# A store of mixed tokens and a weight load move ahead of a store in the SyncE queue of an AdaLN and FFN kernel

## The reference, cut to what matters

```python
# layer 0: grouped 9-tap convolution + context bias, then an int8-quantised matmul
y  = conv1d(x, L0_weight, groups=4) + cond @ c_weight.T + bias
x1 = x + int8_matmul(quantise(y), quantise(L0_ffn_weight)) * scales      # per row
# layer 1: a 64x64 channel mix per batch, then a dense FFN and a gated rank-32 term
x2 = einsum('boi,bih->boh', agg_w[b], x1) + agg_b
H  = x2 @ W.T + b ;  z = x2 @ A
out = x1 + H + (z * gates(H, z)) @ Bmat * scaling
```

## Time and profile before

| | us |
|---|---|
| median of 3 runs (lowest, highest) | 614.74 (613.66, 615.96) |
| the profiled execution | 616.81 |
| its span, first to last instruction | 615.0 |
| PE / DVE / ACT / POOL busy | 599.2 / 434.6 / 356.9 / 374.8 |
| DMA: moved, mean rate | 136.24 MB, 222 GB/s |

### The profile page before, as it was taken

The page is one execution under the profiler, slowest core; times in us unless marked ns, Lnnn a source line. Parts: engine busy times, 40 slices in busy tenths (PEclk is TensorE's granted clock), DMA queues, the critical chain, the costliest instruction groups (busy, mean ns, idle before and its releaser), DMA issues.

```text
span 615.0 us, 16175 instructions
## 1 busy us (share of the span) xinstructions
PE 599.2 (97%) x6467; PEld 343.3 (56%) x6500; DVE 434.6 (71%) x883; ACT 356.9 (58%) x622; POOL 374.8 (61%) x252
## 2 busy tenths in 40 slices
PE   8999999989999999999999999999999999999998
PEld 4656766667767777676554444444444444444444
DVE  5978999978999999997788667654535454355543
ACT  3879998889999999976644343544243333321100
POOL 3326555447766666655797946889877659656200
PEclk8999999999999999999999999999999999999999
DMA  8979988778999898783074115855455346532111
GB/s 339 351 207 297 382 306 295 266 273 299 332 322 328 323 320 314 262 309 139 37 284 163 34 45 193 314 206 194 172 182 200 118 164 237 207 141 99 70 68 69
DMA packets 38632, 136.24 MB, mean 222 GB/s; under 512 B 5036, under 2 KB 5580, under 8 KB 38513
## 3 DMA queue, kind: packets, MB, share of 16 engines
q1 hardware_dynamic: 33518, 118.43, 54.7%
q10 hardware_dynamic: 5040, 16.78, 6.8%
HBM read 87.95 MB, written 47.24 MB: 220 GB/s over the span
## 4 chain that ended last, share of the span: by engine, by line
PE 86%; issue 2%; DVE 1%; ACT 0%; DVEq 0%
PE ps L909 41%; PE ps L612 15%; PE ps L517 9%; PE ps L709 7%; PE ps L596 4%; PE ps L891 2%; PE ps L581 2%; PE ps L657 2%; PE ps L652 1%; PE ps L621 1%; PE ps L625 0%; PE ps L692 0%; DVE yb L1459 0%; PE ps L677 0%; ACT zT L1097 0%
## 5 line engine op out<-in xcount | busy, mean ns | idle before, releaser
L612 PE MATMUL ps<-wqT,yq_both 128*128 128x512 bf16 x479 | 115.2, 378 | 5.6 <-issue 4.6
L1284 POOL TENSOR_TENSOR x<-x_in,f_all 128x512 f32<-128x512 f32 x64 | 74.3, 1161 | 49.4 <-DVE f_all L1496 49.2
L1288 POOL TENSOR_TENSOR x_split<-x_ph,x_split 128x1032 f16<-128x1032 f32 x25 | 53.7, 2148 | 55.5 <-ACT x_split L995 55.5
L1022 ACT ACTIVATE yv<-yb,yinv 128x128 f32<-128x128 f32 x256 | 77.8, 388 | 0.8 <-DVE yinv L1487 0.8
L1323 POOL TENSOR_TENSOR ring<-ring 128x512 f32<-128x512 f32 x56 | 72.7, 1299 | 4.3
L612 PEld LDWEIGHTS ps<-wqT,yq_both 128*128 128x128 bf16 x512 | 45.5, 99 | 46.0 <-issue 1.2
L1496 DVE SCALAR_TENSOR_TENSOR f_all<-ps,tok_scale,wsc_b 128x512 f16<-128x512 f32 x64 | 47.9, 749 | 18.8 <-PE ps L612 17.9
L517 PE MATMUL ps<-x_split,conv_h 128*64 128x256 f16 (+1 forms) x1248 | 60.1, 274 | 0.0
L517 PEld LDWEIGHTS ps<-x_split,conv_h 128*64 128x64 f16 (+1 forms) x1248 | 47.5, 108 | 9.8 <-issue 7.9
L1816 DVE SCALAR_TENSOR_TENSOR x_in<-ps,unscale,x_in 128x512 f32<-128x512 f32 x30 | 22.5, 750 | 39.9 <-PE ps L909 39.8
L1816 DVE SCALAR_TENSOR_TENSOR wst<-ps,unscale,wst 128x512 f32<-128x512 f32 x27 | 20.3, 750 | 36.7 <-PE ps L909 36.7
(11 more groups left out here) (351 smaller groups left out, 1322.2 us busy)
## 6 DMA issues: line engine op xcount, KB each, us to landing
x_in<-in_x SPq DMA_DIRECT2D x32, 512.0 KB, 6.1
x_scratch<-x SPq DMA_DIRECT2D x32, 512.0 KB, 3.6
x_ph<-in_x_phases SPq DMA_DIRECT2D x31, 516.0 KB, 5.1
x_scratch<-ring SPq DMA_DIRECT2D x26, 512.0 KB, 5.2
ring<-x_scratch SPq DMA_DIRECT2D x26, 512.0 KB, 5.4
x_in<-x_scratch SPq DMA_DIRECT2D x12, 512.0 KB, 3.8
out<-x_in ACTq DMA_DIRECT2D x12, 512.0 KB, 3.6
wst<-in_w_rows SPq DMA_DIRECT2D x10, 512.0 KB, 6.7
```

The source lines that it names most:

```text
L612: last = mm(acc_bank(t, h), yqT[:, t % 2, p, :], wqT[:, p, h * HALF:(h + 1) * HALF], start=p == 0, stop=p == PH - 1)
L1022: last = A(yv[:, s, :], yb[:, t % 2, s, :], ACT.Copy, scale=yinv[:, s:s + 1], bias=MAGIC)
L1284: g.tensor_tensor(x1[:, t % 2, s], x_in[:, t % 3, s], f16[:, s], ALU.add).then_inc(sem("x1_ready"), 1)
L1288: g.tensor_tensor(x_split[:, (t - SPLIT) % 2, 1, :], phases(t), x_split[:, (t - SPLIT) % 2, 0, :], ALU.subtract).then_inc(sem("xl_ready"), 1)
```

## The change

In each step of SP's loop, `save_x2(c-4)` moves from behind `save_x1(c-3)` to between `load_phases(c+4)` and `save_x1(c-3)`. `load_ws` moves to right behind `save_x2`, and one step ahead: `load_ws(k)` was in step 12+2k, an even one, and is in step 11+2k, an odd one. No instruction is added or removed, and no wait changes; only the order in SP's queue does.

```diff
                 if c >= 3 and c + LEAD + 1 < NT:
                     load_phases(c + LEAD + 1)
+                if c >= 4 and c - 4 < SAVED:
+                    save_x2(c - 4)
+                if c + 2 in sum_steps:
+                    load_ws(sum_steps.index(c + 2))
                 if c >= 3:
                     save_x1(c - 3)
-                if c >= 4 and c - 4 < SAVED:
-                    save_x2(c - 4)
                 if c == 2:
                     load_phases(4)
                 if 3 <= c < NT:
@@
                 if c + 2 in split_steps:
                     load_w(NL + split_steps.index(c + 2))
-                if c + 1 in sum_steps:
-                    load_ws(sum_steps.index(c + 1))
```

## The result

The changed kernel is slower: 623.27 us median (620.14 to 626.25, 6 runs) against 614.17 us (612.52 to 615.96, 6 runs) for the kernel before on the same chip, a ratio of 1.0138 (95% interval 1.0114 to 1.0162). The profiled execution took 620.14 us with a span of 618.3 us. It is the fastest of the six, and the profiled execution of before (616.81 us) was slower than its median, so the two traces show only a part of the 9.1 us between the medians: 620.14 - 616.81 = 3.3 us. One later execution, in g1_after_again, ran at a granted clock of 0.947 and is left out of every ratio here.

What follows compares the result with a forecast made beforehand. PE was taken to bound the kernel, busy 599.2 of 615.0 us. All terms were 0 except +0.4 us for instruction fetches: 614.74 + 0.4 = 615.1 us, range 611.5 to 618.3 us.

Steps and rivals of the forecast that it cites:

- the fetch term: PE's instruction fetches in the mixes: from -2.2 us (three holes vanish) to +2.7 us (each fetch grows), taken as +0.4 us.
- The zeros: SP's loop: moving the x2 store and the weight load gains and costs 0 us at their readers, x1, x and phases.
- The one open term: PE's idle time called issue, in the mixes: the only term that isn't nothing, +0.4 us, from step 13's fetch.
- the three holes of before: PE's stops amid the mix's 64 small matmuls, 0.24, 0.45 and 1.48 us, read as waits for the next instruction block.
- my own signs of being wrong: In the changed trace: pairs longer than 16.6 us everywhere, ACT waiting for phases, holes gone or in more than three mixes.
- The slower rival: Eight odd steps with a weight load: fetches meet a fuller queue, 3.6 us (618.3 us) to 11.8 us (626.6 us); chance 0.12.

Runs made afterwards that it cites:

- g1_after_again: The changed kernel as it is, run once more: 625.17 us over four runs; the three without the profiled one have ratio 1.0142.
- e1: The kernel before with only the x2 store moved behind the phases, the weight load left in place: 625.08 us, ratio 1.0145.
- f3: The kernel before with 64 small matmuls put in front of PE's first real one: 619.03 us, ratio 1.0058.
- f1: The changed kernel with 32 small matmuls put in front of PE's first real one: 624.72 us, ratio 1.0139.

## Why the prediction was wrong

I had forecast 615.1 us in a range from 611.5 to 618.3 us; it was 623.3 us. The step that failed is the bound of the fetch term, three holes times 0.9 us: it took the wrong price and too few places. Point by point:

- **The zeros were right.** In the loop no engine waits for the phases, for x, x1 or the weights. The x2 store came 1.1 us behind the phases, or 0.6 us in later even steps, and ahead of x1; the x1 store of step 11 went at 110.24 us, where I had said 110.0. An undisturbed pair is 16.5 us. The wait alone (ratio 0.9998) and the weight load alone (1.0015) measured as nothing.
- **The one open term had the right mechanism and the wrong price.** I read the holes as late instruction blocks and saw that the change fills the lull in which they are fetched. Then I priced that by the packet's own length, 0.94 to 1.83 us, and bounded the growth by 0.9 us a fetch. The 1.83 us was no effect of traffic that I could count on: in the changed kernel the packet at 170.4 us takes 0.110 x 8 = 0.88 us, beside data at 98.4%. The packet's length is not what the store ahead of it changes. In step 20 it is 0.93 us in both kernels, and the packet starts 2.3 us later. The time waiting to start has no row of its own in the DMA view; I could have bounded it from the gap in step 20, whose packet of before begins just when the data has drained, by what would now stand in that gap: up to the transfer of one store.
- **I counted only the holes that were there.** "At worst each fetch grows, 3 x 0.9" took the three holes of before as the only places; "holes in more than three mixes" was among my own signs of being wrong. Most of the damage came where before had no hole. In step 20 PE reaches the end of the block 2.9 us into the step, and before, the block had come some 0.6 us earlier (an estimate: the packet's start at 186.01 us plus 2.2 us). Steps 16, 20 and 24 cost 1.28 + 2.39 + 1.29 = 5.0 us; the three old holes changed by +0.55, +0.28 and -1.48 us, and one of 1.61 us came in step 4. A count of PE's instructions in the trace gives the places: block ends recur every 256, and in these three steps they fall 40 to 42 matmuls into the mix. It gives more places than holes, though: a block ends in the mix of 15 of the steps 3 to 29, and the changed kernel's trace has a hole in six.
- **The slower rival came true in its mechanism, in the wrong place.** It had a fuller queue and a deciding point of three holes of 1.48 us, but I hung it on the eight steps with a weight load. That load alone does nothing; the x2 store of the even steps 16, 20 and 24 does. My argument against it, that the undisturbed pairs show no hole with six transfers, missed that their burst comes behind x1, and the lull ahead of it was what saved them. Its chance of 0.12 rested on that argument.
- **The profiled execution's share.** The two traces differ by 3.3 us: +5.0 (steps 16, 20, 24), +0.8 (8, 9), -1.8 (13), -0.3 (6) and -0.4 from an earlier start of the loop, up to which the hole of step 4 (1.6 us) and the stretch at a lower clock in before (1.6 us, below) set each other off. The rest of the 9.1 us between medians is 2.6 us by which the profiled execution of before lay above its median of 614.17 us, and 3.1 us by which that of the changed kernel lay below its own.

**The clock has a part in this rest.** In the trace of before it was granted at 0.50, its lower level of 1.2 GHz, from 10.45 to 13.87 us, after PE had stood idle for 2.00 us; the same matmuls then took 4.60 us, against 2.98 us in the changed kernel's trace, so this stretch cost 1.6 us. First the row of that stretch, then the matmuls before and changed:

```profile
10.50:13.80 3.30, 3.30 (x24) 1.29 (x20) 1.54 (x3) 0.28 (x1) 1.12 (x1) 0.50 1.02 416
```

```profile
9.40 4.60 PE L542 MATMUL ps<-x_ph,conv_w 128*64 128x256 f32 x32 [2.00 <-DMA conv_w<-in_conv_taps]
8.75 2.98 PE L542 MATMUL ps<-x_ph,conv_w 128*64 128x256 f32 x32 [0.82 <-DMA conv_w<-in_conv_taps]
```

That one stretch makes its mean clock 0.997. Of the six executions of the changed kernel the profiled one and one other had a clock of 1.0, two had 0.997 and two 0.995, which is one and two such stretches if they are alike: by an estimate from these rows, 1.6 us each. The two at 0.995 were the two slowest, 625.88 and 626.25 us; in e1 the runs at 1.0, 0.995, 0.992 and 0.989 took 621.39, 623.06, 627.10 and 630.16 us; of the 56 runs of before beside these experiments one had under 0.999. So a fallen clock is more frequent in kernels that have more holes, but it isn't one with them: f3, with four holes in its trace, has 0.997 in six of ten, and f1 has one execution of 626.64 us at 1.0. In the trace of g1 it fell to 0.50 from 132.48 to 135.89 us, right behind the longest hole:

```profile
132.39 1.02 PE L596 MATMUL ps<-mix_home,x 64*64 64x64 f32 x29 [2.77 <-issue]
```

But the 2.15 us hole of the changed kernel's trace has no such fall behind it, and for the other executions there is no trace that shows where theirs stand. That further holes and falls of the clock behind them make up the rest is likely, but not shown.

What stays open: when a block is asked for. My idea of it failed in the shift by 64 instructions. The traces narrow it. After 360 us, in both kernels, every packet starts when PE stands 151 to 196 instructions past a multiple of 256, which is 298 to 253 instructions ahead of the place where it would stop without the block. If a block is asked for no later than that in the loop too, the one of step 20 was due at 180.4 us before and 180.0 us in the changed kernel, ahead of the load of phases, and its packet started 5.6 and 8.3 us later; that it is so in the loop isn't shown. Nor is it shown by what rule the packet waits behind the data: it starts beside data at 97.7% in the changed kernel, so it doesn't need empty engines. That its wait grows with the bytes of the store is shown by three amounts (none, half, all).

The Trainium skill's page "Runtime: NRT & Kernel Launch", section "Instruction fetch mechanics", has blocks of 16 KiB or 256 instructions; the trace agrees, with 0.85 MB in 52 packets and holes at one position of 256 (193 or 194). That the fetch is hidden doesn't hold here: the kernel lost up to 2.15 us at one block end.

## What to carry to other kernels

A stretch in which the DMA engines run empty can be in use: look for the packets of the instruction queue in it before you fill it. A large transfer that nobody waits for still costs, if it stands ahead of such a packet and the engine's code goes by fast where a block ends (here a mix, 64 matmuls and as many weight loads, in 1.10 us). Price a transfer's neighbours by how much later they start, and look for places that are only just in time as well as for those that already stall.

## What the runs showed of the hardware

PE stopped in straight code without any semaphore, for up to 2.15 us in the two kernels' traces, always at the same position of 256 of its instructions; each of these stops ended 2.2 to 2.5 us after the start of a packet of the instruction queue (six holes of the changed kernel, three of before). For all 71 holes of the 13 traces it was 2.2 to 2.9 us. A 512 KB store issued ahead moved the start of such a packet by 2.8 us, half of it by 1.5 us. 64 repeated waits on a semaphore already reached took 3.4 us at PE's start and made 32 instructions in the trace. The granted clock fell to 0.50 for 3.4 us, and 32 matmuls took 4.60 instead of 2.98 us.
